# Recurrent mix: one pipeline of 64 state rows, with the next batch's preparation and the last batch's norm at fixed rows

## The reference

```python
xx = shifted(x) - x                       # the previous token less this one
m  = tanh((x + xx * maa_x) @ w1)          # 4 mixes of rank 32
xw, xk, xv, xr = (x + xx * (maa_f + m_f @ w2_f) for f in "wkvr")
r, k, v = xr @ W_r, xk @ W_k, xv @ W_v
w = exp(-exp(decay + tanh(xw @ dw1) @ dw2))
for t:                                    # for each head
    y_t = r_t . (S + u * k_t v_t)
    S   = w_t * S + k_t v_t
y = layernorm(y) * g + b
out = y @ W_o
```

## Time and profile before

| | us |
|---|---|
| median of 3 runs (lowest, highest) | 2843.17 (2833.26, 2844.16) |
| the profiled execution | 2825.35 |
| its span | 2823.6 |
| recurrent mix, from the first shift to the last residual | 2108.17 to 2332.02 |
| first scan starts; last scan ends | 2132.45; 2318.10 |
| mean granted TensorE clock over the span | 0.936 |

### The profile page before, as it was taken

One profiled execution on the slowest core, in us unless ns is written; L12 is line 12 of the kernel. 1 busy time (PEld: TensorE's weight loads), 2 busy tenths in 40 slices (PEclk: granted clock), 3 DMA queues, 4 the chain that ended last, 5 costly groups with the idle time before them and its releaser, 6 DMA issues. The chain is left out here.

```text
span 2823.6 us, 64040 instructions
## 1 busy us (share of the span) xinstructions
PE 2414.3 (86%) x25809; PEld 1592.7 (56%) x25861; DVE 2072.8 (73%) x3811; ACT 1585.3 (56%) x4088; POOL 264.2 (9%) x278
## 2 busy tenths in 40 slices
PE   6888888888888888888985999999987877999777
PEld 5676676666666776664433666666542322332376
DVE  6899999898999889982033777787626765885465
ACT  3566666666666666663243777777631113677344
POOL 0000000000000000000020110100002432110342
PEclk9999999999999999998996999999988998999889
DMA  5111111111101111102008999898310003220421
GB/s 187 32 33 32 24 25 32 32 32 32 32 21 29 32 32 32 32 2 71 0 22 218 232 234 240 228 249 226 95 38 0 0 0 107 70 76 17 176 69 65
DMA packets 205728, 219.50 MB, mean 78 GB/s; under 512 B 32966, under 2 KB 191447, under 8 KB 199991
## 3 DMA queue, kind: packets, MB, share of 16 engines
q1 hardware_dynamic: 203033, 210.44, 28.5%
q0 software_dynamic: 2400, 4.95, 0.5%
HBM read 137.96 MB, written 79.79 MB: 77 GB/s over the span
## 5 line engine op out<-in xcount | busy, mean ns | idle before, releaser
L2876 DVE TENSOR_REDUCE dl_ZO<-dl_XP 128x64 f32<-128x128 f32 (+6 forms) x448 | 219.8, 491 | 15.4
L1990 ACT ACTIVATE da_AB<-ps 128x384 f32<-128x384 f32 x256 | 124.5, 490 | 142.6 <-PE ps L1851 139.0
L2143 DVE TENSOR_TENSOR ps<-ps,da_window 128x192 f32<-128x192 f32 (+1 forms) x256 | 101.2, 395 | 118.3 <-PE ps L1874 114.0
L2451 PE MATMUL ps<-dl_ST,ident 128*128 128x512 f32 x416 | 187.9, 595 | 0.0
L2871 DVE TENSOR_TENSOR dl_XP<-dl_ZO,dl_G 128x128 f32<-128x128 f32 (+5 forms) x384 | 177.1, 461 | 13.2
L1470 DVE TENSOR_REDUCE ra_top<-ps 128x1 f32<-128x512 f32 x256 | 159.3, 680 | 36.3 <-PE ps L1236 22.8
L2000 ACT ACTIVATE da_E<-ps,da_top 128x512 f32<-128x512 f32 x256 | 176.1, 688 | 17.4 <-DVE da_top L2146 17.0
L2146 DVE TENSOR_REDUCE da_top<-ps 128x1 f32<-128x512 f32 x256 | 176.9, 691 | 8.8
L1370 ACT ACTIVATE ra_PT<-ps 128x512 f32<-128x512 f32 x256 | 135.9, 602 | 61.2 <-PE ps L1267 59.3
L1881 PE MATMUL ps<-ident,da_E 128*128 128x128 f32 x1024 | 168.9, 288 | 1.3 <-ACT da_E L2000 1.2
L2385 PEld LDWEIGHTS ps<-X,dl_taps_v 128*128 128x128 f32 x1088 | 141.4, 211 | 16.0 <-issue 10.7
(11 more groups left out here) (410 smaller groups left out, 5880.6 us busy)
## 6 DMA issues: line engine op xcount, KB each, us to landing
da_bands<-da_AB SPq DMA_DIRECT2D x128, 384.0 KB, 3.8
dl_Abc<-dl_ends SPq DMA_DIRECT2D x64, 512.0 KB, 6.4
da_window<-da_bands SPq DMA_DIRECT2D x128, 192.0 KB, 4.4
da_across<-da_bands SPq DMA_DIRECT2D x128, 192.0 KB, 4.4
da_parts<-da_split SPq DMA_DIRECT2D x64, 96.0 KB, 3.4
ra_parts<-ra_split SPq DMA_DIRECT2D x16, 384.0 KB, 3.7
rf_We<-in_rf_We SPq DMA_DIRECT2D x1, 4608.0 KB, 23.7
da_K<-da_parts SPq DMA_DIRECT2D x16, 256.0 KB
```

The costliest lines, as they stand in the source:

```text
L1990: eng.activation(AB[:, j % STAGES, h, :, :], ps[:, band_bank(v), 0:2 * BAND].rearrange("p (k x) -> p k x", k=2), ACT.Copy)\
L2451: eng.matmul(ps[:, UPDATES[r], :], c.ident[:, :], quarters[:, r, :, :], start=True, stop=alone)
L2876: link(eng.tensor_reduce(ZO[:, to:to + 1 + (2 * I - 1) * CH:CH].rearrange("p (k i) -> p k i", k=2), XP[:, :, :, SB - 1 - t:], AXX, ALU.add))
```

## The change

Only `rwkv_attention` changes. The computation is the same. rkv, wd and we get two copies each (by batch), `centred` and the first Exp's result get tensors of their own. Of the PSUM banks, three now hold the rows (0 to 2, by the running row number g = 16 b + j), one the sums (3), one the tail (4), one the small projections (5), and two are taken in turn by mixes, k, v, r and the own term (6 and 7). The 64 rows run as one sequence. The preparation of batch b+1 and the tail of batch b-1 are issued between the rows of batch b, at row numbers that are written out. On TensorE the spread of row g comes first, then the work fixed at row j, then the sum of row g-3; on VectorE the product of row g+1, the scan of row g, then the work fixed at row j. In the diff below, TensorE's functions come first, then TensorE's order, ScalarE's tail and VectorE's order. The four mixes go in two pairs through the two banks. ScalarE's tail gets one table preload ahead of Ln and Exp.

```diff
+        PES, ACTS, STEPS = 11, 7, 12
+        SUMS, TAIL, SMALL = c.ps[:, 3, :], c.ps[:, 4, :], 5
+        def row(g):
+            return c.ps[:, g % 3, :]
+        def turn(n):
+            return c.ps[:, 6 + n % 2, :]
...
+            def later_mixes(b):
+                eng.wait_ge(chain, b * STEPS + 3)
+                mix_of(b, 3, 0)
+                eng.wait_ge(chain, b * STEPS + 4)
+                mix_of(b, 0, 1)
+            def values(b):
+                eng.wait_ge(chain, b * STEPS + 6)
+                eng.matmul(turn(0), Wrkv[:, 1, :], mix[:, 2, :], start=True, stop=True).then_inc(pe_done, 1)
+            def keys(b):
+                eng.wait_ge(chain, b * STEPS + 8)
...
+            def own_weights(b):
                 eng.wait_ge(chain, b * STEPS + 11)
...
+            def spread_row(g):
+                b, j = g // HS, g % HS
+                if j == 0:
+                    eng.wait_ge(act_done, b * ACTS + 2)
+                if g >= 3:
+                    eng.wait_ge(scanned, g - 2)
+                eng.matmul(row(g), spread[:, j, :], rkv[:, b % 2, 1, :], start=True, stop=True).then_inc(spreads, 1)
+            def sums(g):
+                b, j = g // HS, g % HS
+                if j == 0 and b:
+                    eng.wait_ge(yo, 2 * b - 1)
+                eng.wait_ge(read, g + 1)
+                eng.matmul(SUMS, gather[:, j, :], rS[:, j % DEEP, :], start=j == 0, stop=j == HS - 1).then_inc(summed, 1)
...
+                for j in range(HS):
+                    g = b * HS + j
+                    spread_row(g)
+                    if following and j == 1:
+                        tokens_mixed(b + 1)
+                    if following and j == 3:
+                        first_mixes(b + 1)
+                    if tail and j == 4:
+                        mean(b - 1)
+                    if following and j == 5:
+                        later_mixes(b + 1)
+                    if tail and j == 6:
+                        variance(b - 1)
+                    if following and j == 7:
+                        values(b + 1)
+                    if following and j == 8:
+                        keys(b + 1)
+                    if following and j == 10:
+                        receptance(b + 1)
+                        decay_down(b + 1)
+                    if following and j == 11:
+                        decay_up(b + 1)
+                    if tail and j == 12:
+                        output(b - 1)
+                    if following and j == 13:
+                        own_weights(b + 1)
+                    if g >= BEHIND:
+                        sums(g - BEHIND)
...
             def deviation(b):
+                eng.preload_act_table_set("natural_log_exp_and_others")
...
+                for j in range(HS):
+                    if b * HS + j + 1 < B * HS:
+                        products(b * HS + j + 1)
+                    scan(b, j)
+                    if following and j == 0:
+                        shift(b + 1)
+                    if tail and j == 2:
+                        sum_up(b - 1)
+                    if following and j == 4:
+                        scale_mix(b + 1, 2, 2)
+                        scale_mix(b + 1, 1, 3)
+                    if tail and j == 5:
+                        centre(b - 1)
+                    if following and j == 5:
+                        add_tokens(b + 1, 2, 3)
+                    if following and j == 6:
+                        scale_mix(b + 1, 3, 4)
+                        scale_mix(b + 1, 0, 5)
+                    if following and j == 7:
+                        add_tokens(b + 1, 1, 4)
+                        add_tokens(b + 1, 3, 6)
+                    if following and j == 8:
+                        add_tokens(b + 1, 0, 7)
+                    if tail and j == 9:
+                        scale_norm(b - 1)
+                    if tail and j == 10:
+                        shift_norm(b - 1)
+                    if following and j == 12:
+                        own_keys(b + 1)
+                    if tail and j == 13:
+                        residual(b - 1)
+                    if following and j == 14:
+                        own_values(b + 1)
```

More of the change, by code:

```diff
@@ L820, in rwkv_attention @@
     pe_done, act_done = c.sem("rw_pe"), c.sem("rw_act")
-    vb_ready, kv_ready, scanned, read, summed = (c.sem("rw_" + n) for n in ("vb", "kv", "scanned", "read", "summed"))
+    spreads, keyed, scanned, read, summed = (c.sem("rw_" + n) for n in ("spreads", "keyed", "scanned", "read", "summed"))
     ym, yc, ys, yv, yl, yr, yn, yo = (c.sem("rw_y" + n) for n in "mcsvlrno")
@@ L837, in rwkv_attention @@
         mix = c.sb("rw_mix", [P, 4, T], ctx)
[L838 to L839 removed]
+        rkv = c.sb("rw_rkv", [P, 2, 3, T], ctx)
+        wd = c.sb("rw_wd", [P, 2, T], ctx)
         wt = c.sb("rw_wt", [64, T], ctx)
[L841 removed]
+        power = c.sb("rw_power", [P, T], ctx)
+        we = c.sb("rw_we", [P, 2, T], ctx)
         ruk = c.sb("rw_ruk", [P, T], ctx)
@@ L886, in states @@
[L886 to L896, removed]
+                if b:
+                    eng.wait_ge(act_done, b * ACTS - 1)
@@ new lines, in tokens_mixed, with mix_of, first_mixes @@
+                eng.matmul(c.ps[:, SMALL, :], w1[:, :], xxx[:, :], start=True, stop=True).then_inc(pe_done, 1)
+            def mix_of(b, f, bank):
+                eng.matmul(turn(bank), w2[32 * f:32 * f + 32, :], m[32 * f:32 * f + 32, :], start=True, stop=True).then_inc(pe_done, 1)
+            def first_mixes(b):
+                eng.wait_ge(act_done, b * ACTS + 1)
+                eng.wait_ge(chain, b * STEPS)
+                mix_of(b, 2, 0)
+                mix_of(b, 1, 1)
+            def later_mixes(b):
[3 more added lines that the diff above has]
+                mix_of(b, 0, 1)
@@ new lines, in values, with receptance @@
+            def values(b):
[3 more added lines that the diff above has]
+                eng.wait_ge(chain, b * STEPS + 8)
+                eng.matmul(turn(1), Wrkv[:, 0, :], mix[:, 1, :], start=True, stop=True).then_inc(pe_done, 1)
+            def receptance(b):
+                eng.wait_ge(chain, b * STEPS + 9)
+                eng.wait_ge(act_done, b * ACTS + 2)
+                eng.matmul(turn(0), Wrkv[:, 2, :], mix[:, 3, :], start=True, stop=True).then_inc(pe_done, 1)
@@ new lines, in decay_down, with decay_up @@
+            def decay_down(b):
+                eng.wait_ge(chain, b * STEPS + 10)
+                eng.matmul(c.ps[0:64, SMALL, :], dw1[:, :], mix[:, 0, :], start=True, stop=True).then_inc(pe_done, 1)
+            def decay_up(b):
+                eng.wait_ge(act_done, b * ACTS + 5)
+                eng.matmul(c.ps[:, SMALL, :], dw2[:, :], wt[:, :], start=True, stop=True).then_inc(pe_done, 1)
+            def own_weights(b):
+                eng.wait_ge(chain, b * STEPS + 11)
+                eng.matmul(turn(1), heads[:, :], ruk[:, :], start=True, stop=True).then_inc(pe_done, 1)
@@ L911, in _ @@
             tokens_mixed(0)
-            four_mixes(0)
-            projections(0)
-            for b in range(B):
[L915 to L924, removed]
+            first_mixes(0)
+            later_mixes(0)
+            values(0)
+            keys(0)
+            receptance(0)
+            decay_down(0)
+            decay_up(0)
+            own_weights(0)
+            for b in range(B):
+                following, tail = b + 1 < B, b > 0
+                for j in range(HS):
[26 more added lines that the diff above has]
+                        sums(g - BEHIND)
+            for g in range(B * HS - BEHIND, B * HS):
+                sums(g)
+            mean(B - 1)
+            variance(B - 1)
+            output(B - 1)
         @block.scalar
@@ L929, in squash @@
                 eng.wait_ge(pe_done, b * PES + 1)
-                eng.activation(m[:, :], c.ps[:, 7, :], ACT.Tanh).then_inc(act_done, 1)
-            def decays(b):
[L933 to L942, removed]
+                eng.activation(m[:, :], c.ps[:, SMALL, :], ACT.Tanh).then_inc(act_done, 1)
@@ new lines, in copy_values, with copy_keys, copy_receptance @@
+            def copy_values(b):
+                eng.wait_ge(pe_done, b * PES + 6)
+                if b >= 2:
+                    eng.wait_ge(scanned, HS * (b - 1))
+                eng.activation(rkv[:, b % 2, 1, :], turn(0), ACT.Copy).then_inc(act_done, 1)
+            def copy_keys(b):
+                eng.wait_ge(pe_done, b * PES + 7)
+                eng.activation(rkv[:, b % 2, 0, :], turn(1), ACT.Copy).then_inc(act_done, 1)
+            def copy_receptance(b):
+                eng.wait_ge(pe_done, b * PES + 8)
+                if b >= 2:
+                    eng.wait_ge(read, HS * (b - 1))
+                eng.activation(rkv[:, b % 2, 2, :], turn(0), ACT.Copy).then_inc(act_done, 1)
@@ L955, in _ @@
             squash(0)
+            copy_values(0)
+            copy_keys(0)
+            copy_receptance(0)
             decays(0)
             for b in range(B):
```

(73 more changed lines are left out.)

40 lines of the change are left out of this document (14 added, 26 removed).

## The result

| | us |
|---|---|
| before, median of its runs beside this | 2843.66 (2833.26 to 2850.07) |
| after, median | 2896.09 (2886.53 to 2903.48) |
| ratio after / before | 1.0194 (95% interval 1.0164 to 1.0224) |
| profiled execution after, its span | 2903.48, 2901.7 |
| mix, first shift to last residual: before, after | 223.8, 281.2 |

The change costs 52 us by the medians and 57.4 us inside the mix in the two profiles. (The rest of the difference between the two profiled executions lies in the layers around it; the first shift starts 7.4 us later in the one after.) The forecast was +44 us, to 2887.

The account below looks back on a forecast made before the run. The mix was taken as bound by VectorE in scans and a TensorE, ScalarE, VectorE chain in gaps. Loop +25.4, preparation -2, tail -1.3 and clock +22 gave about +44 us: 2887 us, range 2850 to 2906.

Parts of the forecast that it names:

- The order in TensorE's queue: Scan rows: VectorE's next spread stands behind a TensorE matmul waiting for VectorE's previous row; three matmuls cost 3.02 us.
- Seven places: Mixed tokens, first sum, later mixes, variance, values, keys, own weights: TensorE waits on the row before; 57.0 us.
- The worked-out 66.9 us: Added waits in the loop: 57.0 us at seven places plus 9.9 at four more matmuls.
- variance and keys: Waits at rows 6 and 8 of a batch, three times each: 9.8 and 7.2 us in all.
- +25.4 for the loop: First to last scan at unchanged clock: VectorE's 144.2 us plus 66.9 of waits, 211.1 against 185.65.
- The clock: TensorE's clock falls after idle spells in the loop: 12 of 18 spells at 1.85 us each, +22 us.
- rival 2: VectorE's added operations in the scan rows also meet GpSimd's multiply: +8.9 us, so 2896; chance 0.15.
- TensorE's idle spells: 18 waits, six places three times each, while VectorE does product, scan and awaited operation: 2.5 to 3.3 us each.
- Preparation and tail: Before the first scan, earlier value projection: -2 us; after the last, one table preload: -1.3 us.
- Rival 1: TensorE's clock holds through the loop, leaving only the waits: +22 us, 2865; chance 0.18.
- Rival 3: TensorE runs further ahead or round trips overlap: half the waits, -12 to +10 us, near 2845; chance 0.11.
- Rival 4: Banks let TensorE stay ahead, only VectorE's work counts: loop 144.2, gain 45 us, 2798; chance 0.09.

Follow-up runs that it names:

- the second run with the clock held: Repeat of the changed kernel with TensorE filling six waits of a batch with matmuls on constant data; 2866.21 us.
- the filled kernel: The changed kernel, with two or three matmuls on constant data filling six TensorE waits of a batch; 2863.79 us, ratio to before 1.0076.
- the last kernel: The changed kernel reordered: TensorE's inputs made at least three rows earlier, sums in two banks and four rows behind; 2793.13 us, ratio to before 0.9836.

## Why the prediction was right

- The order in TensorE's queue: right. Seven places, three waits at each, all of VectorE's idle time before one line. The worked-out 66.9 us came to 64.9 and 63.8 at a held clock. Two of the waits, variance and keys, were taken too long by 4.3 us in all, because the adds that GpSimd lengthened run beside them; without that the sum would be some 68. The term was +25.4 for the loop; with the clock held it is 214.2 to 215.3 less 185.7, or +28.5 to +29.6.
- The clock: right in kind, too small. I took two falls in three, 22 us, of 33 at most; the runs show 32. Too few falls were counted, while the price of one was about right: against the second run with the clock held, the stall is longer by 1.0 to 2.8 us at 16 of the 18 places, 2.0 in the mean where I had 1.85, and equal at two (the values in batch 0, the own weights in batch 1). The round trip shown above is 5.58 where I had 3.02.
- GpSimd (rival 2): the mechanism holds, its price does not. VectorE's operations take 6.3 us more than its 144.2, where I held the work unchanged in the forecast and priced the rival at 8.9; but some 4 us of the lengthening are hidden in the round trips, and only the shift's 2.6 count. The Trainium skill (SBUF — State Buffer, Who interferes with whom) said that the later of the two waits for the whole of the other; the trace agrees in 1633 ns against 752. That the rival's 2896 is the measured 2896.09 is a coincidence: the 9 us above the forecast come mostly from the clock.
- TensorE's idle spells: forecast at 2.5 to 3.3 us, they are 2.5 to 3.1 at five of the six places in the mean, but 4.7 before the mixed tokens, where the held-up shift adds to them.
- Preparation and tail: -2 and -1.3 worked out; 21.07 against 24.28 is -3.2, and 12.71 against 13.92 is -1.2.
- The sum in the profiles: 61.8 (loop) - 3.2 - 1.2 = +57.4 against +44. Of the 13 between, 10 are the clock's and 3 to 4 the rest of the loop, less 1 for the preparation. By the medians it is +52; the profiled execution before was faster than the median of its kernel, the one after slower.
- Rival 1 (the clock holds) is what the filled kernel shows, +22 and +29 us in its two runs where the rival was priced at +22; the change itself does not do it. Rival 3 fell: the waits are whole. Rival 4, faster at 2798 since only VectorE's own work counts, is wrong for this order and right for the one with three rows between (2793): its condition, that TensorE's input is ready when TensorE gets there, was the point. So the Trainium skill's advice to interleave stretches with different limits (Perfetto Trace Analysis, Optimization Strategy) holds in the traces only under that condition: this order of the same work lost 52 us, and the one with three rows between gained 47.

The clock was not held at one place alone, so whether a fall at one place brings on the next stays open, and so does what the added row and the separate bank for the sums each bring in the last kernel.

## What to carry to other kernels

Before work is put between the steps of a pipeline, list for each piece where its input is made and what is queued behind it on its engine. If the input is made one step earlier on the engine that needs the next item of that queue, the two engines take turns, at the price of a whole round trip; put as many steps between as the round trip has (here three matmuls, 2.94 us, over rows of 1.72: one step left 97 us of stalls, two left 33, and three, with a second bank for the sums, 6). Hidden work that is spread over a busy stretch can also break up TensorE's own activity, and its clock (0.83 in this loop, against 0.95 before) then makes each round trip dearer; an operation that is lengthened behind the awaited one may cost nothing, while the delay of one that is itself awaited counts in full (2.6 us here, worked out from the stalls).

## What the runs showed of the hardware

GpSimd holds up an operation with one SBUF tensor too. In the last kernel the norm's shift, a TENSOR_SCALAR second behind a scan, took 1.37 us beside the multiply in all three batches, where the same operation first behind a scan took 0.46 in the change. The place behind the operation whose result it reads is not the reason: in that kernel's last tail, where it follows the same operation and GpSimd has nothing left to multiply, it took 0.49. VectorE and GpSimd there:

```profile
2188.85 0.73 DVE L1121 SCALAR_TENSOR_TENSOR rw_own<-rw_centred,rw_maa,rw_Q 128x512 f32<-128x512 f32 x1
2189.61 1.37 DVE L1125 TENSOR_SCALAR rw_Y<-rw_own,rw_maa 128x512 f32<-128x512 f32 x1
...
2282.00 0.49 DVE L1125 TENSOR_SCALAR rw_Y<-rw_own,rw_maa 128x512 f32<-128x512 f32 x1
```

```profile
2189.07 1.63 POOL L1063 TENSOR_TENSOR rw_rS<-rw_rkv,rw_S 128x512 f32<-128x512 f32 x1 [1.49 <-ACT rw_wt L1013]
```

The multiply is recorded from 2189.07 to 2190.70, and the shift ends at 2190.98, some 0.28 later.
